# A three-layer graph network on one core: 13 extraction rounds, gathers over 104 partitions, and a reordered preparation

## The chip, the cores and the metric

The kernel runs on one core of one Trainium2 chip. The metric is the device time of one execution in microseconds. Five engines work side by side and wait for each other through semaphores: TensorE (PE), VectorE (DVE), ScalarE (ACT), GpSimd (POOL) and SyncE (SP, which issues most DMAs).

## The reference

A GraphSAGE network of three layers over 100000 nodes and 150000 edges (50000 drawn ones and one loop per node), sorted by destination. Neighbour rows are averaged over the in-degree.

```python
deg = segment_sum(ones, dst); inv_deg = where(deg > 0, 1 / maximum(deg, 1), 0)[:, None]
def sage(h, w_self, w_neigh, b):
    agg = segment_sum(h[src], dst) * inv_deg
    return h @ w_self + agg @ w_neigh + b
h = maximum(layernorm(x), 0)          # x: [100000, 128]
h = relu(sage(h, ws0, wn0, b0))       # 128 -> 256
h = relu(sage(h, ws1, wn1, b1))       # 256 -> 256
out = x + sage(h, ws2, wn2, b2)       # 256 -> 128
```

## The kernel before

**Tiles.** Nodes are cut into tiles of 128. Each node's own loop is handled apart, so that a tile has some 64 other edges. Layers 0 and 1 go over 392 pairs of tiles, layer 2 over 264 triples. For each tile one indirect DMA of GpSimd gathers the source rows of its edges, one edge per partition, and TensorE adds them up by destination with a 0/1 matrix (`select`). A partition with no edge has a row number out of bounds: its row is skipped, and what stands in the buffer (zeroed once) is multiplied by zero. Layer 0 gathers rows of `x` (512 bytes, L581), layer 1 rows of `p_rows` (1024 bytes, L595), layer 2 rows of `z_rows` (512 bytes, L608), two gathers per pair or triple. Buffers have four slots; each engine has its own hand-ordered loop.

**Preparation.** Ahead of layer 0 the kernel makes the edge lists. SyncE loads every 60th destination (`starts_b`, 2500 numbers copied to 114 partitions), the destinations (`dst_all`, `dst_next`), the weights and the biases. VectorE and ScalarE count, for seven chunks of 114 tiles each, where a tile's edges begin (`below`, `row_index`; ScalarE by the sum of a Sign, L638). GpSimd fetches a window of 300 edges per tile (`win_mem`, seven indirect DMAs of 114 rows, L519). Meanwhile the weights are split into two parts, `w_hi` by ScalarE (L641) and `w_lo` by VectorE (L848). Then each of a tile's edges gets a number (`wf_key`), 0 for foreign edges and own loops. Extraction takes the largest eight numbers of each tile with MAX8 (L874) and deletes them with MATCH_REPLACE8 (L878), seven tiles of chunks a round, `ROUNDS` = 14 rounds, so at most 112 edges a tile. TensorE turns the result (`keys`) so that edges lie on partitions. Out of it come `slot_index` (which row to gather), `slot_node` (which node in the tile it belongs to, from `node_i` and `empty_t`) and, for layer 2, the triple tables.

**The flag.** Six tests of the input (order, windows long enough, the last extracted slot empty, and so on) go into `faults`, are summed by TensorE, and set `general_flag`. If it is not 0, a slow general path for arbitrary inputs is taken. Each engine loads the flag and branches; GpSimd and ScalarE did so twice before layer 0, first around the general sums, then between the two forms of layer 0. SyncE's loads of `x`, GpSimd's gathers and all of layer 0 begin behind the flag.

Of the kernel before, what the change touches and what calls it, by code (L numbers as in the profile page):

```python
# [9 lines left out]
ALU = mybir.AluOpType  # L10
ACT = mybir.ActivationFunctionType
# [31 lines left out]
ROUNDS = 14  # L43
# [49 lines left out]
def build(nc, x, src, dst, dst_starts, windows, ws0, wn0, b0, ws1, wn1, b1, ws2, wn2, b2, out):  # L93
# [13 lines left out]
    with ExitStack() as ctx:  # L107
# [3 lines left out]
        def sem(name):  # L111
            return ctx.enter_context(nc.semaphore(name))
# [184 lines left out]
        prep = sem("prep")  # L297
        keys_ready, keys_taken, keys_turned = sem("keys_ready"), sem("keys_taken"), sem("keys_turned")
# [206 lines left out]
        def _(pool):  # L505
# [20 lines left out]

            def general(pass_no):
                table, sums, width = GENERAL[pass_no]
                with pool.If(pool.value_load(general_flag[0:1, 0:1], min_val=0, max_val=1) != 0):
                    if pass_no == 0:  # L530
                        pool.memset(zero_rows[:, :], 0.0).then_inc(ge_zero_made, 1)

                        pool.iota(slot_index[:, :], pattern=[[P, TILES]], base=0, channel_multiplier=1
                                  ).then_inc(ge_index_set, 1)
                    pool.wait_ge(ge_cleared, pass_no + 1)
                    with_degree = pass_no == 0
                    puts = 2 if with_degree else 1
                    with pool.Fori(0, EW) as i:
                        pool.wait_ge(ge_index, i + (pass_no * EW + 1))
                        pool.sem_inc(pool_may_go, 1)  # L540
                        pool.indirect_dma_start(ge_msg[:, 0:width], None, table,
                                                bass.IndirectOffsetOnAxis(ge_src[:, :], axis=0),
                                                bounds_check=last_row, oob_is_err=False).then_inc(ge_fetched[pass_no], 16)
                        pool.indirect_dma_start(ge_cur[:, 0:width], None, sums,
                                                bass.IndirectOffsetOnAxis(ge_at[:, :], axis=0),
                                                bounds_check=last_row, oob_is_err=False).then_inc(ge_fetched[pass_no], 16)
                        if with_degree:
                            pool.indirect_dma_start(ge_deg[:, :], None, degree_dram,
                                                    bass.IndirectOffsetOnAxis(ge_at[:, :], axis=0),
                                                    bounds_check=N_ROWS - 1, oob_is_err=False  # L550
                                                    ).then_inc(ge_fetched[pass_no], 16)
                        pool.wait_ge(ge_new_ready, i + (pass_no * EW + 1))
                        pool.sem_inc(pool_may_go, 1)
                        pool.indirect_dma_start(sums, bass.IndirectOffsetOnAxis(ge_put_at[:, :], axis=0),
                                                ge_new[:, 0:width], None,
                                                bounds_check=last_row, oob_is_err=False).then_inc(ge_put[pass_no], 16)
                        if with_degree:
                            pool.indirect_dma_start(degree_dram, bass.IndirectOffsetOnAxis(ge_put_at[:, :], axis=0),
                                                    ge_deg_new[:, :], None,
                                                    bounds_check=N_ROWS - 1, oob_is_err=False).then_inc(ge_put[pass_no], 16)  # L560
                        pool.wait_ge(ge_put[pass_no], i * (16 * puts) + 16 * puts)
                        pool.sem_inc(pool_may_go, 1)
                    if pass_no == 0:
                        pool.wait_ge(ge_index_set, 1)

            def layer0_gathers(table):
                def step(first):
                    if first.live():
                        if first.has(SLOTS):
                            pool.wait_ge(L0.gathered[first.slot], first.use * 32)  # L570
                        pool.tensor_copy(gather_at[first.slot][:, 0:2], slot_index[:, bass.ds(first.n * 2, 2)]
                                         ).then_inc(L0.index_copied, 1)
                    s = first.back(1)
                    if s.live():
                        if s.has(SLOTS):

                            pool.wait_ge(L0.normed, s.back(SLOTS).n + 1)
                        pool.wait_ge(L0.index_copied, s.n + 1)
                        pool.sem_inc(pool_may_go, 1)
                        for j in range(2):  # L580
                            pool.indirect_dma_start(raw[s.slot][:, 2 + j, :], None, table,  # L581
                                                    bass.IndirectOffsetOnAxis(gather_at[s.slot][:, j:j + 1], axis=0),
                                                    bounds_check=last_row, oob_is_err=False
                                                    ).then_inc(L0.gathered[s.slot], 16)
                pipeline(pool, step, PAIRS, 1)

            def gathers(layer, table, rows_in, freed, width):
                def gather(s):
                    if s.has(SLOTS):

                        pool.wait_ge(freed, s.back(SLOTS).n + 1)
                    pool.wait_ge(layer.index_copied, s.n + 1)
                    pool.sem_inc(pool_may_go, 1)
                    for j in range(2):
                        pool.indirect_dma_start(rows_in[s.slot][:, j, 0:width], None, table,  # L595
                                                bass.IndirectOffsetOnAxis(gather_at[s.slot][:, j:j + 1], axis=0),
                                                bounds_check=last_row, oob_is_err=False
                                                ).then_inc(layer.gathered[s.slot], 16)
                pipeline(pool, gather, PAIRS, 0)
# [32 lines left out]
        def _(act):  # L632
            act.wait_ge(const_made, 1)
            act.wait_ge(starts_loaded, 16)
# [17 lines left out]
            act.activation(wf_next, wf_loop, ACT.Copy, accum_out=loop_count[:, :]).then_inc(loops_counted, 1)  # L652

# [5 lines left out]
            act.wait_ge(flag_set, 1)  # L659
            with act.If(flagged()):  # L660
                with act.Fori(0, EW) as i:
                    act.wait_ge(ge_var_ready, i + 1)
                    act.activation(ge_std[:, :], ge_moments[:, 1:2], ACT.Sqrt, bias=eps_col[0:EP, :]
                                   ).then_inc(ge_std_ready, 1)
# [66 lines left out]
            act.wait_ge(nbr_cleared, SLOTS + 3)  # L731
            with act.If(flagged()):
                pipeline(act, layer0(True), PAIRS, 5)
                act.wait_ge(ge_nodes_off, 1)
# [60 lines left out]
        def _(dve):  # L795
# [86 lines left out]
            for j in range(SHARED):  # L882
                for q in range(SHARED_CHUNKS):
# [13 lines left out]
            own_step(dve.tensor_scalar(empty_t[:, :], keys_t[:, :], 0.0, -float(SENTINEL), op0=ALU.is_equal,  # L897
                                       op1=ALU.mult))

            dve.tensor_scalar(slot_index[:, :], key_i[:, :], 7, None, op0=ALU.logical_shift_right)  # L900
            own_step(dve.tensor_scalar(node_i[:, :], key_i[:, :], P - 1, None, op0=ALU.bitwise_and))
            own_step(dve.tensor_tensor(slot_node[:, :], node_i[:, :], empty_t[:, :], ALU.add))
# [11 lines left out]
            dve.reduce_max(faults[:, 5:6], shared_empty[:, :], AX.X).then_inc(faults_ready, 1)  # L914
            dve.wait_ge(faults_summed, 1)
# [4 lines left out]

            own_step(dve.tensor_tensor(keys_t[:, 0:n_own], keys_t[:, 0:n_own], shared_t[:, :], ALU.add))
# [503 lines left out]
```

## Time and profile before

| | us |
|---|---|
| median of 3 runs | 3935.56 |
| lowest, highest | 3934.75, 3937.95 |
| the profiled execution | 3934.27 |
| its span, first to last instruction | 3932.1 |
| preparation, to the first statistics of layer 0 | 142.2 |
| first and last gather of layer 1 start | 2165.4, 3214.8 |

Over the span PE is busy 3513.3 us (89%), DVE 3546.8 (90%), ACT 3016.1 (77%), POOL 2277.0 (58%). The granted TensorE clock is 0.933 of full speed in the mean; it is at full speed through layer 0.

How to read it: a row in order of time has the start in us from the span's start, the duration in us, the engine, the line, what it writes and reads, and in brackets how long the engine had been idle and what released it ("issue" means nothing that the profile shows). "x7" merges seven like instructions. SPq is SyncE's queue issuing a DMA; the row's duration is the issue, not the transfer. A DMA_INDIRECT row of POOL is the time in which GpSimd writes the gather's descriptors.

### The profile page before, as it was taken

What the parts mean: (1) busy time and instruction counts of PE and PEld (TensorE: products, weight loads), DVE (VectorE), ACT (ScalarE), POOL (GpSimd) and SP (SyncE); (2) the same over time, 40 slices, a digit from 0 to 9 for tenths busy, and PEclk for the clock granted to TensorE, in tenths of its full rate; (3) what the DMA queues carried; (4) which work ended last, traced back from release to release, by engine and by line L of the source; (5) the groups of instructions that cost most, each with busy time, mean ns of one, the idle gap of its engine ahead of it and who ended that gap; (6) DMA issues with size and microseconds to landing.
All of it is one profiled execution on the core that took longest, in us unless ns stands there. A gap on an engine that the chain in (4) does not pass through costs nothing. (4 is left out here: it accounts for less than half of the span.)

```text
span 3932.1 us, 111274 instructions
## 1 busy us (share of the span) xinstructions
PE 3513.3 (89%) x22511; PEld 3171.6 (81%) x22511; DVE 3546.8 (90%) x12529; ACT 3016.1 (77%) x8011; POOL 2277.0 (58%) x2513
## 2 busy tenths in 40 slices
PE   0499999999999999999999899999999987776666
PEld 0488888888888888888888799999999986666565
DVE  8899999999999999999998788888888877777777
ACT  2488888888888888888886778778778767777777
POOL 1344444444444444444442777777777767777776
PEclk9999999999999999999999999999999996666666
DMA  1144444444444444444444788888888878999998
GB/s 55 56 142 139 141 143 142 139 140 144 142 140 140 143 142 139 140 144 141 139 140 139 215 244 246 244 246 247 242 243 244 242 223 256 264 264 266 265 263 251
DMA packets 1040774, 727.06 MB, mean 185 GB/s; under 512 B 103208, under 2 KB 1012656, under 8 KB 1040632
## 3 DMA queue, kind: packets, MB, share of 16 engines
q1 hardware_dynamic: 854298, 569.93, 48.2%
q0 software_dynamic: 80848, 104.93, 10.7%
q10 hardware_dynamic: 105600, 51.92, 4.4%
q14 instruction: 22, 0.18, 0.0%
q8 instruction: 6, 0.10, 0.0%
HBM read 451.60 MB, written 360.71 MB: 207 GB/s over the span
## 5 line engine op out<-in xcount | busy, mean ns | idle before, releaser
L581 POOL DMA_INDIRECT loaded_rows<-in_x,gather_at x784 | 859.2, 1096 | 1047.6 <-ACT h_nbr L691 906.5
L1269 PE MATMUL ps_out<-w_hi,hid_hi 128*128 128x512 f32 (+1 forms) x3136 | 1120.6, 357 | 29.9 <-DVE layer_mem L1173 28.2
L1269 PE MATMUL ps_out<-w_hi,hid_lo 128*128 128x512 f32 (+1 forms) x3136 | 1066.3, 340 | 0.0
L1269 PE MATMUL ps_out<-w_lo,hid_hi 128*128 128x512 f32 (+1 forms) x3136 | 1061.9, 339 | 0.0
L595 POOL DMA_INDIRECT layer_mem<-p_rows,gather_at x784 | 804.1, 1026 | 289.2 <-issue 216.0
L1269 PEld LDWEIGHTS ps_out<-w_hi,hid_hi 128*128 128x128 f32 x3136 | 590.8, 188 | 139.4 <-issue 39.7
L1269 PEld LDWEIGHTS ps_out<-w_hi,hid_lo 128*128 128x128 f32 x3136 | 588.7, 188 | 72.5
L1269 PEld LDWEIGHTS ps_out<-w_lo,hid_hi 128*128 128x128 f32 x3136 | 592.8, 189 | 60.7
L608 POOL DMA_INDIRECT layer_mem<-z_rows,gather_at x528 | 525.8, 996 | 181.3 <-issue 140.8
L721 ACT ACTIVATE cat_hi<-ps_turn 128x512 fp32r<-128x512 f32 x392 | 236.0, 602 | 375.3 <-PE ps_turn L1306 373.9
L1269 PE MATMUL ps_hid<-cat_hi,w_hi 128*128 128x256 f32 x1568 | 472.0, 301 | 0.0
L780 ACT ACTIVATE layer_mem<-iota_row,triple_node 128x128 f32<-128x128 f32 x1056 | 337.3, 390 | 150.9 <-DVE stored_rows L1215 77.9
L1269 PE MATMUL ps_hid<-cat_lo,w_hi 128*128 128x256 f32 x1568 | 439.3, 280 | 0.0
L1269 PE MATMUL ps_hid<-cat_hi,w_lo 128*128 128x256 f32 x1568 | 438.9, 280 | 0.0
L1162 DVE SCALAR_TENSOR_TENSOR hid_lo<-ps_out,hid_hi 128x512 fp32r<-128x512 f32 x392 | 270.3, 690 | 111.0 <-ACT hid_hi L769 101.3
L691 ACT ACTIVATE h_own<-loaded_rows,shift,rstd 128x128 f32<-128x128 f32 x784 | 340.7, 484 | 2.0 <-DVE shift L1130 2.0
L1063 DVE BATCH_NORM_STATS2 stats<-loaded_rows 128x6 f32<-128x128 f32 x1568 | 338.1, 278 | 4.0 <-DMA loaded_rows<-in_x,gather_at 4.0
L691 ACT ACTIVATE h_nbr<-loaded_rows,shift,rstd 128x128 f32<-128x128 f32 x784 | 341.3, 484 | 0.0
L1107 DVE SCALAR_TENSOR_TENSOR layer_mem<-stored_rows,self_scale,ps_out 128x256 f32<-128x256 f32 x784 | 339.6, 475 | 0.1
L673 ACT ACTIVATE nbr_hi<-layer_mem 128x256 fp32r<-128x256 f32 x392 | 163.1, 416 | 229.9 <-DMA layer_mem<-p_rows,gather_at 227.4
L713 ACT ACTIVATE layer_mem<-ps_hid,b_col 128x256 f32<-128x256 f32 x784 | 320.7, 461 | 1.0 <-DVE hid_lo L1097 0.7
L1269 PEld LDWEIGHTS ps_hid<-cat_lo,w_hi 128*128 128x128 f32 x1568 | 296.6, 189 | 0.0
(162 smaller groups left out, 8783.6 us busy)
## 6 DMA issues: line engine op xcount, KB each, us to landing
p_rows<-stored_rows SPq DMA_DIRECT2D x392, 256.0 KB, 2.2
q_rows<-layer_mem SPq DMA_DIRECT2D x392, 256.0 KB, 2.6
loaded_rows<-q_rows SPq DMA_DIRECT2D x392, 256.0 KB
loaded_rows<-y_rows SPq DMA_DIRECT2D x264, 192.0 KB
layer_mem<-in_x SPq DMA_DIRECT2D x264, 192.0 KB
out_rows<-stored_rows ACTq DMA_DIRECT2D x264, 192.0 KB
loaded_rows<-in_x SPq DMA_DIRECT2D x392, 128.0 KB, 2.6
z_rows<-layer_mem SPq DMA_DIRECT2D x392, 128.0 KB
```

Source lines behind the costliest of these rows:

```text
L581: pool.indirect_dma_start(raw[s.slot][:, 2 + j, :], None, table, bass.IndirectOffsetOnAxis(gather_at[s.slot][:, j:j + 1], axis=0), bounds_ ...
L595: pool.indirect_dma_start(rows_in[s.slot][:, j, 0:width], None, table, bass.IndirectOffsetOnAxis(gather_at[s.slot][:, j:j + 1], axis=0), b ...
L608: pool.indirect_dma_start(triple_rows_in[s.slot][:, j, :], None, z_dram, bass.IndirectOffsetOnAxis(gather_at[s.slot][:, j:j + 1], axis=0), ...
L673: act.activation(nbr_hi[s.half][:, 0:tiles, 0:width], nbr[s.slot][:, 0:tiles, 0:width], ACT.Copy).then_inc(layer.nbr_hi_ready, 1)
L691: last = act.activation(rows, raw[t.slot][:, j, :], ACT.Relu, bias=shift[t.half][:, j:j + 1], scale=rstd[t.half][:, j:j + 1])
L713: last = act.activation(h1[t.half][:, m, :], ps_hid[t.half][:, m * PAIR:(m + 1) * PAIR], ACT.Relu, bias=b0_col[:, m:m + 1])
L721: act.activation(cat_hi[t.half][:, :, :], ps_turn[:, :].rearrange("p (k n) -> p k n", k=2), ACT.Copy).then_inc(L0.hi_ready, 1)
L780: last = act.activation(triple_distance[s.half][:, b, :], iota_row[:, :], ACT.Abs, scale=-1.0, bias=triple_node[:, bass.ds(s.n * (2 * SHAR ...
L1063: last = dve.bn_stats(stats[t.half][:, j, :], raw[t.slot][:, j, :])
L1107: last = dve.scalar_tensor_tensor(q_out[t.slot][:, j, :], p_out[t.slot][:, j, :], self_scale[:, bass.ds(t.n * 2 + j, 1)], ps_out[t.half][: ...
L1162: dve.scalar_tensor_tensor(hid_lo[t.half][:, :, :], l1_turn[t.half].rearrange("p (k n) -> p k n", k=2), 0.0, hid_hi[t.half][:, :, :].bitca ...
L1269: ins = nc.tensor.matmul(o, a, b, start=n == 0, stop=n == len(terms) - 1)
```

## The change

1. `ROUNDS` goes from 14 to 13; the gathers of layers 0 and 1 (plain path) take partitions 0 to `SLOT_ROWS` - 1 = 103 of the buffer and of the row numbers, where they took all 128. Layer 2 keeps 128.
2. SyncE waits for `starts_b` before it issues any other load. ScalarE runs a one-column Sign on an unused tile first.
3. ScalarE copies 342 of the 798 columns of `keys_t` beside VectorE's copy of 456. `empty_t` is made while TensorE sums the faults; `node_i` and `slot_node` are made behind the flag.
4. GpSimd and ScalarE test the flag once before layer 0: the general sums move into the branch that chooses the form of layer 0. (`general_sums` is the old body of `general`, unchanged.)

```diff
-ROUNDS = 14
+ROUNDS = 13
+SLOT_ROWS = 8 * ROUNDS
@@ sync
             sp.dma_start(starts_b, ...).then_inc(starts_loaded, 16)
+            sp.wait_ge(starts_loaded, 16)
             sp.dma_start(dst_all[:, :], dst_flat).then_inc(dst_loaded, 16)
@@ gpsimd: layer0_gathers(table, rows), gathers(...)
-                            pool.indirect_dma_start(raw[s.slot][:, 2 + j, :], None, table,
-                                                    bass.IndirectOffsetOnAxis(gather_at[s.slot][:, j:j + 1], axis=0),
+                            pool.indirect_dma_start(raw[s.slot][0:rows, 2 + j, :], None, table,
+                                                    bass.IndirectOffsetOnAxis(gather_at[s.slot][0:rows, j:j + 1], axis=0),
...
-                        pool.indirect_dma_start(rows_in[s.slot][:, j, 0:width], None, table,
+                        pool.indirect_dma_start(rows_in[s.slot][0:SLOT_ROWS, j, 0:width], None, table,
...
-            general(0)
             with pool.If(pool.value_load(general_flag[0:1, 0:1], min_val=0, max_val=1) != 0):
-                layer0_gathers(h0_sums)
+                general_sums(0)
+                layer0_gathers(h0_sums, P)
             with pool.Else():
-                layer0_gathers(x)
+                layer0_gathers(x, SLOT_ROWS)
@@ scalar
             act.wait_ge(const_made, 1)
+            act.activation(ge_alone[:, :], eps_col[:, :], ACT.Sign)
             act.wait_ge(starts_loaded, 16)
...
+            act.wait_ge(keys_turned, 1)
+            act.activation(keys_t[:, 4 * TP:TILES], l1_turn[1][:, 0:(CHUNKS - 4) * TP], ACT.Copy).then_inc(keys_copied, 1)
@@ vector
-            dve.tensor_copy(keys_t[:, 0:4 * TP], l1_turn[0][:, 0:4 * TP])
-            own_step(dve.tensor_copy(keys_t[:, 4 * TP:TILES], l1_turn[1][:, 0:(CHUNKS - 4) * TP]))
-            dve.tensor_scalar(key_i[:, :], keys_t[:, :], -1.0, None, op0=ALU.add)
+            own_step(dve.tensor_copy(keys_t[:, 0:4 * TP], l1_turn[0][:, 0:4 * TP]))
+            dve.wait_ge(keys_copied, 1)
+            own_step(dve.tensor_scalar(key_i[:, :], keys_t[:, :], -1.0, None, op0=ALU.add))
```

VectorE from the turned keys to the flag (L918 before, L923 after), before:

```order
L894 COPY keys_t<-ps_out 128x456 [waits keys_turned]
L895 COPY keys_t<-ps_out 128x342
L896 TENSOR_SCALAR key_i<-keys_t 128x798 [waits prep]
L897 TENSOR_SCALAR empty_t<-keys_t 128x798
L900 TENSOR_SCALAR slot_index<-key_i 128x798 [waits prep]
L901 TENSOR_SCALAR node_i<-key_i 128x798
L902 TENSOR_TENSOR slot_node<-node_i,empty_t 128x798 [waits prep]
...
L912 SCALAR_TENSOR_TENSOR layer_mem<-keys_t,layer_mem 128x528 [waits prep]
L914 TENSOR_REDUCE faults<-layer_mem 128x1 [waits prep]
L916 TENSOR_REDUCE fault_sum<-ps_out 128x1 [waits faults_summed]
L917 TENSOR_SCALAR fast<-fault_sum 128x1 [waits prep]
L918 TENSOR_SCALAR general_flag<-fault_sum 1x1
```

and after:

```order
L902 COPY keys_t<-ps_out 128x456 [waits keys_turned]
L904 TENSOR_SCALAR key_i<-keys_t 128x798 [waits keys_copied,prep]
L905 TENSOR_SCALAR slot_index<-key_i 128x798 [waits prep]
L912 COPY layer_mem<-ps_hid 128x264 [waits shared_turned]
L912 COPY layer_mem<-ps_hid 128x264
L915 SCALAR_TENSOR_TENSOR layer_mem<-keys_t,layer_mem 128x528 [waits prep]
L917 TENSOR_REDUCE faults<-layer_mem 128x1 [waits prep]
L918 TENSOR_SCALAR empty_t<-keys_t 128x798
L921 TENSOR_REDUCE fault_sum<-ps_out 128x1 [waits faults_summed,prep]
L922 TENSOR_SCALAR fast<-fault_sum 128x1 [waits prep]
L923 TENSOR_SCALAR general_flag<-fault_sum 1x1
```

`empty_t` stands behind the instruction that hands the faults to TensorE, `node_i` and `slot_node` behind the flag, and one copy of two is gone.

GpSimd from the window gathers to the first gather of layer 0 (left out are the general path and its form of layer 0), before:

```order
L529 TENSOR_LOAD general_flag [waits nbr_cleared,flag_set]
L529 ISA x2
L529 COMPARE_AND_BRANCH
...
L616 TENSOR_LOAD general_flag
L616 ISA x2
L616 COMPARE_AND_BRANCH
...
L616 UNCONDITIONAL_BRANCH
L571 COPY gather_at<-slot_index 128x2 x2
L581 DMA loaded_rows<-in_x,gather_at 128x128 [waits index_copied_0]
L581 DMA loaded_rows<-in_x,gather_at 128x128
```

and after:

```order
L621 TENSOR_LOAD general_flag [waits nbr_cleared,flag_set]
L621 ISA x2
L621 COMPARE_AND_BRANCH
...
L621 UNCONDITIONAL_BRANCH
L577 COPY gather_at<-slot_index 128x2 x2
L587 DMA loaded_rows<-in_x,gather_at 104x128 [waits index_copied_0]
L587 DMA loaded_rows<-in_x,gather_at 104x128
```

One load of the flag with its branch is gone, and the gather writes 104 partitions.

SyncE's first loads, before:

```order
L395 DMA layer_mem<-in_dst_starts 114x2500
L397 DMA dst_all<-in_dst 125x1200
L398 DMA dst_next<-in_dst 124x2
L399 DMA b_col<-in_L_gnn_b 128x2x1
L400 DMA layer_mem<-in_L_gnn_ws 128x256
```

and after:

```order
L397 DMA layer_mem<-in_dst_starts 114x2500
L400 DMA dst_all<-in_dst 125x1200 [waits starts_loaded]
L401 DMA dst_next<-in_dst 124x2
L402 DMA b_col<-in_L_gnn_b 128x2x1
L403 DMA layer_mem<-in_L_gnn_ws 128x256
```

The second load now waits for the first to land.

## Rows read from the trace of the kernel before

**Rows 1.** Busy time per engine (count), TensorE clock, DMA; layers 0, 1.

```profile
400.00:2150.00 1750.00, 1750.00 (x10964) 1560.36 (x10963) 1724.41 (x6821) 1418.89 (x3759) 806.16 (x1013) 1.00 0.47 141
2250.00:3200.00 950.00, 924.32 (x7087) 870.42 (x7086) 844.35 (x2481) 757.64 (x2125) 726.65 (x708) 1.00 0.84 245
```

**Rows 2.** GpSimd's gathers by line: busy, mean ns, idle before; last row min/median/max ns.

```profile
L581 POOL DMA_INDIRECT loaded_rows<-in_x,gather_at x674 | 740.0, 1098 | 914.9 <-ACT h_nbr L691 795.0 <-issue 113.9 <-POOL gather_at L571 6.0
...
L595 POOL DMA_INDIRECT layer_mem<-p_rows,gather_at x708 | 726.7, 1026 | 223.5 <-issue 156.2 <-DVE gather_at L1027 44.4 <-PE ps_hid L1341 12.2
...
L595 POOL DMA_INDIRECT layer_mem<-p_rows,gather_at x784: 992/998/1340, 2165.4 to 3214.8; - x196
```

**Rows 3.** In order of time: start, us, engine, line; VectorE, two extraction rounds.

```profile
82.35 2.69 DVE L874 MAX8 keys<-wf_key_mem 114x8 f32<-114x300 f32 x7
...
88.03 2.69 DVE L874 MAX8 keys<-wf_key_mem 114x8 f32<-114x300 f32 x7
```

**Rows 4.** In order of time, the first 32 us, several engines.

```profile
11.23 2.82 DVE L831 TENSOR_SCALAR_CACHE_REDUCE layer_mem<-layer_mem,tile_base 114x2500 f32<-114x2500 int32 x1 [6.00 <-DMA layer_mem<-in_dst_starts]
...
11.27 1.28 ACT L638 ACT_TABLE_LOAD   x1 [11.27 <-DMA layer_mem<-in_dst_starts]
...
13.67 1.26 SPq L406 DMA_DIRECT2D layer_mem<-in_L_gnn_ws  x1
...
15.07 0.15 DVE L828 TENSOR_SCALAR row_index<-below 114x1 int32<-114x1 f32 x1 [0.64 <-ACT layer_mem L638]
...
22.46 1.89 ACT L641 ACTIVATE w_hi<-layer_mem 128x2048 fp32r<-128x2048 f32 x1
...
27.10 2.29 DVE L848 TENSOR_TENSOR w_lo<-layer_mem,w_hi 128x2048 fp32r<-128x2048 f32 x1
...
31.68 2.35 DVE L854 TENSOR_TENSOR layer_mem<-win_mem 114x2100 f32<-114x2100 int32 x1 [2.28 <-DMA win_mem<-in_windows,row_index]
```

**Rows 5.** DMA view, 0:12 and 12:32 us: packets, MB; us to landing.

```profile
q1 hardware_dynamic: 551, 1.54, 36.8%
...
layer_mem<-in_L_gnn_ws SPq DMA_DIRECT2D x1, 128.0 KB, 6.0
```

**Rows 6.** In order of time, VectorE from keys to flag.

```profile
127.10 0.50 DVE L895 COPY keys_t<-ps_out 128x342 f32<-128x342 f32 x1
...
128.13 0.57 DVE L897 TENSOR_SCALAR empty_t<-keys_t 128x798 f32<-128x798 f32 x1
...
129.83 0.99 DVE L902 TENSOR_TENSOR slot_node<-node_i,empty_t 128x798 f32<-128x798 int32 x1
...
133.80 0.17 DVE L916 TENSOR_REDUCE fault_sum<-ps_out 128x1 f32<-128x8 f32 x1 [0.69 <-PE ps_out L1238]
...
134.07 0.13 DVE L918 TENSOR_SCALAR general_flag<-fault_sum 1x1 int32<-1x1 f32 x1
```

**Rows 7.** In order of time, from flag to first pair of layer 0.

```profile
135.29 2.14 SPq L464 DMA_DIRECT2D loaded_rows<-in_x  x4
...
136.37 0.70 POOL L571 COPY gather_at<-slot_index 128x2 int32<-128x2 int32 x2 [108.31 <-issue]
...
137.58 1.84 POOL L581 DMA_INDIRECT loaded_rows<-in_x,gather_at  x1 [0.51 <-POOL gather_at L571]
...
139.73 1.00 POOL L581 DMA_INDIRECT loaded_rows<-in_x,gather_at  x1 [0.30 <-issue]
...
142.22 0.87 DVE L1063 BATCH_NORM_STATS2 stats<-loaded_rows 128x6 f32<-128x128 f32 x4 [3.59 <-DMA loaded_rows<-in_x,gather_at]
```

**Rows 8.** In order of time, GpSimd, the last window gather.

```profile
26.88 1.19 POOL L519 DMA_INDIRECT win_mem<-in_windows,row_index  x1 [0.30 <-issue]
```

**Rows 9.** Gather queue's packets, MB: 400:2150, 2250:3200, 12:32 us.

```profile
q0 software_dynamic: 21600, 22.24, 6.0%
...
q0 software_dynamic: 33978, 46.60, 18.7%
...
q0 software_dynamic: 1232, 1.92, 32.0%
```

More of the change, by code:

```diff
@@ L297, in build @@
         prep = sem("prep")
+        keys_copied = sem("keys_copied")
         keys_ready, keys_taken, keys_turned = sem("keys_ready"), sem("keys_taken"), sem("keys_turned")
@@ L525, in _, with general_sums @@
             last_row = pool.snap(limit)
+            def general_sums(pass_no):
+                table, sums, width = GENERAL[pass_no]
+                if pass_no == 0:
+                    pool.memset(zero_rows[:, :], 0.0).then_inc(ge_zero_made, 1)
+                    pool.iota(slot_index[:, :], pattern=[[P, TILES]], base=0, channel_multiplier=1
+                              ).then_inc(ge_index_set, 1)
+                pool.wait_ge(ge_cleared, pass_no + 1)
+                with_degree = pass_no == 0
+                puts = 2 if with_degree else 1
+                with pool.Fori(0, EW) as i:
+                    pool.wait_ge(ge_index, i + (pass_no * EW + 1))
+                    pool.sem_inc(pool_may_go, 1)
+                    pool.indirect_dma_start(ge_msg[:, 0:width], None, table,
+                                            bass.IndirectOffsetOnAxis(ge_src[:, :], axis=0),
+                                            bounds_check=last_row, oob_is_err=False).then_inc(ge_fetched[pass_no], 16)
+                    pool.indirect_dma_start(ge_cur[:, 0:width], None, sums,
+                                            bass.IndirectOffsetOnAxis(ge_at[:, :], axis=0),
+                                            bounds_check=last_row, oob_is_err=False).then_inc(ge_fetched[pass_no], 16)
+                    if with_degree:
+                        pool.indirect_dma_start(ge_deg[:, :], None, degree_dram,
+                                                bass.IndirectOffsetOnAxis(ge_at[:, :], axis=0),
+                                                bounds_check=N_ROWS - 1, oob_is_err=False
+                                                ).then_inc(ge_fetched[pass_no], 16)
+                    pool.wait_ge(ge_new_ready, i + (pass_no * EW + 1))
+                    pool.sem_inc(pool_may_go, 1)
+                    pool.indirect_dma_start(sums, bass.IndirectOffsetOnAxis(ge_put_at[:, :], axis=0),
+                                            ge_new[:, 0:width], None,
+                                            bounds_check=last_row, oob_is_err=False).then_inc(ge_put[pass_no], 16)
+                    if with_degree:
+                        pool.indirect_dma_start(degree_dram, bass.IndirectOffsetOnAxis(ge_put_at[:, :], axis=0),
+                                                ge_deg_new[:, :], None,
+                                                bounds_check=N_ROWS - 1, oob_is_err=False).then_inc(ge_put[pass_no], 16)
+                    pool.wait_ge(ge_put[pass_no], i * (16 * puts) + 16 * puts)
+                    pool.sem_inc(pool_may_go, 1)
+                if pass_no == 0:
+                    pool.wait_ge(ge_index_set, 1)
@@ L527, in general @@
             def general(pass_no):
-                table, sums, width = GENERAL[pass_no]
                 with pool.If(pool.value_load(general_flag[0:1, 0:1], min_val=0, max_val=1) != 0):
[L530 to L564, printed above, removed]
@@ L566, in layer0_gathers @@
-            def layer0_gathers(table):
+                    general_sums(pass_no)
+            def layer0_gathers(table, rows):
                 def step(first):
@@ L652, in _ @@
             act.activation(wf_next, wf_loop, ACT.Copy, accum_out=loop_count[:, :]).then_inc(loops_counted, 1)
+            act.wait_ge(keys_turned, 1)
+            act.activation(keys_t[:, 4 * TP:TILES], l1_turn[1][:, 0:(CHUNKS - 4) * TP], ACT.Copy).then_inc(keys_copied, 1)
             def flagged():
                 return act.value_load(general_flag[0:1, 0:1], min_val=0, max_val=1) != 0
[L659 to L664, printed above, removed]
             def nbr_hi_part(layer, s, tiles, width):
@@ L731, in _ @@
             act.wait_ge(nbr_cleared, SLOTS + 3)
+            act.wait_ge(flag_set, 1)
             with act.If(flagged()):
+                with act.Fori(0, EW) as i:
+                    act.wait_ge(ge_var_ready, i + 1)
+                    act.activation(ge_std[:, :], ge_moments[:, 1:2], ACT.Sqrt, bias=eps_col[0:EP, :]
+                                   ).then_inc(ge_std_ready, 1)
                 pipeline(act, layer0(True), PAIRS, 5)
@@ L914, in _ @@
             dve.reduce_max(faults[:, 5:6], shared_empty[:, :], AX.X).then_inc(faults_ready, 1)
+            own_step(dve.tensor_scalar(empty_t[:, :], keys_t[:, :], 0.0, -float(SENTINEL), op0=ALU.is_equal,
+                                       op1=ALU.mult))
             dve.wait_ge(faults_summed, 1)
@@ L919, in _ @@
             dve.sem_inc(flag_set, 1)
+            own_step(dve.tensor_scalar(node_i[:, :], key_i[:, :], P - 1, None, op0=ALU.bitwise_and))
+            own_step(dve.tensor_tensor(slot_node[:, :], node_i[:, :], empty_t[:, :], ALU.add))
             own_step(dve.tensor_tensor(keys_t[:, 0:n_own], keys_t[:, 0:n_own], shared_t[:, :], ALU.add))
```

6 lines of the change are left out of this document (1 added, 5 removed).

## Prediction

> **What bounds the kernel now.** I read the busy time by stage first, then the gathers' own lines, then the first 145 us in order of time, because the change touches the preparation and the gathers and nothing else. [rows 1] gives the two long stages. In layer 0 TensorE is busy 1750.00 of 1750.00 us, at full clock: it is the bound. In layer 1 TensorE is busy 924.32 of 950.00 us and GpSimd 726.65. That looks like TensorE again, but [rows 2] says otherwise. GpSimd's 708 gathers took 726.7 us and the gaps between them 223.5 us, 950.2 together, so GpSimd never stops in layer 1. The gap is the same 0.3 us after each (223.5 / 708 = 0.316), an issue cost and no wait. The 784 gathers of the layer start between 2165.4 and 3214.8 us, one each 1.34 us. So a hundredth of a microsecond on one layer 1 gather is 7.8 us of kernel. In layer 0 GpSimd is idle 914.9 of 1750 us, most of it waiting for ScalarE to free a buffer: there the gather's length costs nothing. Layer 2 keeps its 128 partitions and is left alone. Ahead of layer 0 stands the preparation, some 142 us of a serial chain through VectorE, in which each step saved comes off the end.
>
> **One round of extraction.** A round is seven MAX8 and seven MATCH_REPLACE8, back to back with no idle time. It starts at 82.35 and the next at 88.03 [rows 3]: 5.68 us. The 14th goes: **-5.7**. The wider zero fill of `keys` is a part of a 0.15 us memset. The limit falls from 111 edges a tile to 103; counted from the inputs, the fullest of the 782 tiles has 89 edges besides its nodes' own loops, so the flag stays 0 and the plain path runs.
>
> **Row numbers alone and first.** VectorE starts its first count at 11.23 us after 6.00 us of idle time, on the landing of `starts_b` [rows 4]. By 12 us the queue had moved 1.54 MB [rows 5], and `starts_b` is 114 x 2500 x 4 bytes, 1.14 MB: at most 0.40 MB of other data went before its end or just behind it. At the mean of 1.54 MB in 12 us that is worth 3.1 us if all of it was in the way, and nothing if it was queued behind. SyncE issued `starts_b` first and one queue serves its transfers in turn, so I take a value near the lower end, **-0.5**, and keep 0 to -2 for the range (some of the 0.40 MB certainly fell in the last microsecond). Below nothing it can't go: nothing new stands ahead of this load.
>
> What is pushed back are the eleven other loads and the padding store; they now start at about 11 us. Before, the last weight load was issued at 13.67 [rows 4] and landed 6.0 us later [rows 5], and its issue had stood behind the big loads draining. With `starts_b` gone I expect it at 16 to 17 us, landed at 22 to 23; at worst it keeps its distance and is issued 11 us later, at 24.7, landed at 30.7. ScalarE is free for `w_hi` at 22.46, or 21.4 with what follows. VectorE takes `w_lo` at 27.10 and idles 2.28 us before the windows come at 31.68 [rows 4]. With 1.89 us for `w_hi` and 2.29 for `w_lo`, both fit if the weights land by 26.4: cover for the likely case, not for the worst, which costs 4.3.
>
> **The table load.** The first Sign of ScalarE loads its table for 1.28 us after the row numbers have come, at 11.27 [rows 4]. The dummy Sign on `ge_alone` does it while ScalarE waits anyway. VectorE waited 0.64 us for the first ScalarE count, at 15.07; later counts were ready. **-0.6**, passed on through `row_index`, GpSimd's seven window gathers and their landing, since the last gather, not the weights, ends the wait at 31.68.
>
> **The way to the flag.** Four steps leave it. The copy L895 (0.5) goes to ScalarE beside VectorE's wider copy; at ScalarE's rate for `w_hi`, 1.89 us for 2048 columns [rows 4], its 342 columns end sooner. `empty_t` L897 (0.6) goes into the 0.69 us in which VectorE waits for the fault sum. `node_i` L901, of the shape of L897, and `slot_node` L902 (0.6 and 1.0) go behind the flag [rows 6]. That is 2.7; what had been overlapped between short instructions and is now a wait costs some 0.2: **-2.5**, the flag at 131.7 where it was 134.2 (on the old clock).
>
> **Behind the flag.** SyncE's first load goes out 1.09 us after the flag (134.20 to 135.29) with one test of the flag; GpSimd's index copy 2.17 us after it (136.37) with two [rows 7]. The merged branch leaves GpSimd one test: **-1.1**. Against it: the first gather took 1.84 us and the second 1.00; beside the first VectorE was making the node tables, beside the second it had stopped at 138.63 [rows 7]. Now `node_i` and `slot_node` fill the gap and both gathers lie beside VectorE, so the second may take 1.84 too: 0 to +0.84, **+0.4**. (The Trainium skill, "SBUF — State Buffer", section "Who interferes with whom", says that VectorE's two-port modes lock GpSimd out of writing descriptors; these two rows agree, the 0.84 us above is theirs.) VectorE is done with its tables at 131.7 + 1.6 + 4.4 = 137.7, before the first pair lands at about 139, so the tables are covered; if the gathers came 1 us sooner they would not be. ScalarE's merged branch ends in idle time.
>
> Sum of the preparation: -5.7 - 0.5 - 0.6 - 2.5 - 1.1 + 0.4 = **-10.0 us**, from -8.3 (row numbers 0, gather +0.84, 0.8 of waits more) to -12. Layers 0 to 2 then run as they did.
>
> **104 partitions.** The rows with no edge carry an index out of range and fetch nothing, before as after, so no bytes go. What could change is GpSimd's time to write a gather. The trace has one other size, the window gathers of 114 rows: 1.19 us against a median of 0.998 [rows 2, 8]. Fewer rows took longer. The queue's packets explain it [rows 9]. Layer 0: 21600 over 674 gathers, 32 = 16 x 2. Layer 1: 33978 over 708, 48 = 16 x 3. Windows: 1232 over 7, 176 = 16 x 11. One of each engine's packets is the completion; the others are 1, 2 and 10, which fit eight rows of 512 bytes, eight of 1024 and 19 of 2400 at up to 4 to 5 KB a packet. So all 16 engines always get a list as long as that of the one with the most rows, and 114 rows were dealt as 6 x 19, where 16 x 8 would have held them. Dealt evenly, 104 is 13 x 8: the list stays at 8. GpSimd's time goes with the list (0.19 us for 11 entries more, 0.017 each), and so stays at 1.00: **0 us** for 784 gathers.
>
> The Trainium skill ("DMA: Bandwidth & Descriptors", section "Why a DMA increments its semaphore by 16 and not by 1", paragraph "How many engines (k)") states the rule outright: the largest k up to 16 that divides the number of partitions. The packet counts agree with it for 114 and 128; no run so far shows 104. By the common reading, that fewer partitions mean less work, the sum would be the -28 us of the first rival below; by this rule it is the -10.0.
>
> The profiled execution took 3934.27 us, span 3932.1; the median of the runs is 3935.56, 1.3 more. 3935.56 - 10.0 = **3925.6 us**.
>
> **Rivals.** *Gathers get shorter.* If time goes with rows or with a list of 104/16, 6.5 rounded to 7, a gather saves 0.017 us (-13 us, 3912), and in proportion to the rows up to 0.19. It can't all be had: TensorE is idle only 25.7 of 950 us of layer 1 [rows 1], 2.7%, so it takes over as the bound after 28 us: 3898. For: nothing but the smaller number. Against: the 114 rows.
>
> *Gathers get longer*, the one that ends slower. Part of the 0.19 us of the window gathers may be not the longer list but the uneven deal itself, a path of the descriptor writer for anything but 16 engines. Layer 1 pays it 784 times with no cover, layer 0 not at all. At 0.013 us it has eaten the 10.0; at the full 0.19 it is +149, 4075. Were 104 dealt as 8 x 13, the list of 13 would give 5 x 0.017 x 784 = +67, 3993. Against: the arithmetic of a list explains the 0.19 alone.
>
> *The preparation gives less.* The loads pushed back meet the window gathers on the queue's engines, and the last window or the weights land 2 to 8 us late (the weights' worst is 4.3): 3928 to 3934. For: weights, edge ends and windows now share 12 to 25 us. Against: the cover above.
>
> **How the numbers follow.** Forecast 0.50 (3923 to 3928). Shorter gathers 0.14, longer 0.22 (a third of it below +30), less preparation 0.14. A measurement of this kernel tells about 0.2% from no change, 7.9 us: faster is below 3927.7. Most of the forecast, the shorter gathers and a little of the last case give 0.60; the last case, the edge of the forecast and a loss of 0.003 to 0.02 us per gather give 0.22; beyond that 0.18. The range takes the forecast, less preparation, shorter gathers to -20 and longer ones to +0.025: **3905 to 3943**.
>
> **What would show it.** In the trace after: rounds still 5.68 us, twelve replaces; ScalarE's table load before 5 us and no 0.64 us wait; flag 9.3 us sooner than 134.2; first statistics at about 132.2 instead of 142.22; layer 1 gathers at a median of 1.00 and one each 1.34 us; the gather queue's packets still 32 and 48 a gather. I am wrong if the layer 1 median moves by over 0.01 us, if the packets a gather change, or if the windows land later than 30.8.

## The result: slower by 1.0%, and the profile after

| | before | changed |
|---|---|---|
| median us | 3936.35 | 3976.19 |
| lowest, highest | 3934.75, 3937.95 | 3974.81, 3978.92 |
| span of the profiled run | 3932.1 | 3976.7 |

The ratio is 1.0102, with a 95% interval of 1.0085 to 1.012: 40 us lost, where 10 gained were forecast. The range ended at 3943. (The column "before" has one run more than the table ahead of the prediction, and with it a median 0.8 us higher.)

The busy times by stretch of the changed kernel, columns as in [rows 1], the first row layer 0, the second layer 1:

```profile
390.00:2140.00 1750.00, 1750.00 (x10967) 1559.71 (x10966) 1724.79 (x6826) 1419.49 (x3760) 833.13 (x1016) 1.00 0.47 141
...
2250.00:3200.00 950.00, 899.93 (x6774) 826.39 (x6772) 814.72 (x2371) 723.05 (x2028) 742.15 (x677) 1.00 0.83 234
```

Layer 0 is as it was: TensorE has no idle time. In layer 1 TensorE fell from 924.32 to 899.93 us of 950, VectorE and ScalarE fell too, and GpSimd rose. The gathers of the changed kernel (layer 0's line, layer 1's line with shortest, median and longest ns and the start of first and last; then layer 1's busy time, mean and idle time before) stand against [rows 2]:

```profile
L587 POOL DMA_INDIRECT loaded_rows<-in_x,gather_at x784: 1076/1090/1254, 129.0 to 2111.5; - x196
...
L601 POOL DMA_INDIRECT layer_mem<-p_rows,gather_at x784: 1077/1082/1432, 2157.3 to 3258.7; - x196
...
L601 POOL DMA_INDIRECT layer_mem<-p_rows,gather_at x677 | 743.2, 1098 | 208.1 <-issue 147.0 <-DVE gather_at L1034 49.2 <-PE ps_hid L1348 6.7
```

The median gather of layer 1 went from 0.998 to 1.082 us, the shortest from 0.992 to 1.077. GpSimd still never stops: 743 us of work and 208 of gaps fill the stretch. First to last start is now 1101.4 us where it was 1049.4: **+52.0**. The first gather of layer 1 starts at 2157.3 instead of 2165.4: **-8.1** from what stands before. The span grew by 44.6, and 52.0 - 8.1 is 43.9 of it.

The gather queue's packets in the same two stretches (packets, MB, share), against [rows 9]:

```profile
q0 software_dynamic: 21632, 22.27, 6.6%
...
q0 software_dynamic: 32458, 44.49, 19.6%
```

Layer 1: 32458 packets over 677 gathers, 47.9 each; 48.0 before. The bytes are the same too, 65.7 and 65.8 KB a gather. By both the queue carries the same lists; the time in which GpSimd writes them is longer.

The preparation of the changed kernel in order of time, against [rows 3, 4, 6, 7]:

```profile
10.56 2.82 DVE L839 TENSOR_SCALAR_CACHE_REDUCE layer_mem<-layer_mem,tile_base 114x2500 f32<-114x2500 int32 x1 [5.33 <-DMA layer_mem<-in_dst_starts]
...
25.71 1.20 POOL L522 DMA_INDIRECT win_mem<-in_windows,row_index  x1 [0.30 <-issue]
...
25.88 1.91 ACT L648 ACTIVATE w_hi<-layer_mem 128x2048 fp32r<-128x2048 f32 x1 [5.33 <-DMA layer_mem<-in_L_gnn_ws]
...
31.87 2.35 DVE L862 TENSOR_TENSOR layer_mem<-win_mem 114x2100 f32<-114x2100 int32 x1 [1.68 <-DMA win_mem<-in_windows,row_index]
...
116.68 2.69 DVE L882 MAX8 keys<-wf_key_mem 114x8 f32<-114x300 f32 x7
...
125.89 0.17 DVE L921 TENSOR_REDUCE fault_sum<-ps_out 128x1 f32<-128x8 f32 x1 [0.27 <-PE ps_out L1245]
...
126.17 0.13 DVE L923 TENSOR_SCALAR general_flag<-fault_sum 1x1 int32<-1x1 f32 x1
...
127.73 0.48 POOL L577 COPY gather_at<-slot_index 128x2 int32<-128x2 int32 x2 [100.82 <-issue]
...
129.01 1.21 POOL L587 DMA_INDIRECT loaded_rows<-in_x,gather_at  x1 [0.79 <-POOL gather_at L577]
...
130.53 1.22 POOL L587 DMA_INDIRECT loaded_rows<-in_x,gather_at  x1 [0.30 <-issue]
...
133.70 0.87 DVE L1070 BATCH_NORM_STATS2 stats<-loaded_rows 128x6 f32<-128x128 f32 x4 [1.32 <-DMA loaded_rows<-in_x,gather_at]
```

### The profile page after: what moved, and what is told of

Same layout as the page of the kernel before. It is cut to its first block and busy times, and to the rows that moved or that the text cites. A ratio compares the mean times of both kernels' runs of the same rounds, so it can differ in the third digit from the quotient of the medians.

```text
span 3976.7 us, 111247 instructions
## 1 busy us (share of the span) xinstructions
PE 3532.3 (89%) x22511; PEld 3167.0 (80%) x22511; DVE 3549.9 (89%) x12507; ACT 3016.5 (76%) x8013; POOL 2364.0 (59%) x2513
## 5 line engine op out<-in xcount | busy, mean ns | idle before, releaser
L587 POOL DMA_INDIRECT loaded_rows<-in_x,gather_at x784 | 890.2, 1136 | 1014.8 <-ACT h_nbr L694 874.2
L1276 PE MATMUL ps_out<-w_hi,hid_hi 128*128 128x512 f32 (+1 forms) x3136 | 1111.5, 354 | 59.4 <-DVE layer_mem L1180 55.9
L601 POOL DMA_INDIRECT layer_mem<-p_rows,gather_at x784 | 860.9, 1098 | 284.3 <-issue 216.2
```

The source lines that it names most:

```text
L587: pool.indirect_dma_start(raw[s.slot][0:rows, 2 + j, :], None, table, bass.IndirectOffsetOnAxis(gather_at[s.slot][0:rows, j:j + 1], axis=0 ...
L601: pool.indirect_dma_start(rows_in[s.slot][0:SLOT_ROWS, j, 0:width], None, table, bass.IndirectOffsetOnAxis(gather_at[s.slot][0:SLOT_ROWS, ...
L1276: ins = nc.tensor.matmul(o, a, b, start=n == 0, stop=n == len(terms) - 1)
```

## Experiments

Two theories stood against each other on the gather. **A**: the loss is in the gather over 104 partitions alone, and in it a price for any number of partitions that isn't dealt over all 16 DMA engines. **Rivals**: something else in the change slows layer 1; or any gather over fewer than 128 partitions pays; or the price goes with the number of engines left out.

### Both gathers back at 128 partitions

```diff
-SLOT_ROWS = 8 * ROUNDS
+SLOT_ROWS = P
```

> The changed kernel with the gathers of layers 0 and 1 back over 128 partitions, all else kept. Theory A (the loss is the gather over 104 partitions and nothing else): layer 1 median back at 0.998 us, one gather each 1.34 us, its 784 gathers in 1050 us where the changed kernel took 1102; time 3976 - 52 = 3924 to 3928, which is before less the 8.5 us that the preparation gained. Rival (something else of the change, such as the shorter preparation or the merged branch, slows layer 1): the gathers stay near 1.08 us and the time near 3970.

Measured: 4350.61 us where the kernel before took 4359.51, ratio 0.998 (0.997 to 0.9989). These times need a word. This run, the kernel with eight sizes and the first runs with 112 and with 96 partitions were on another chip, on which layers 1 and 2 took longer. Layer 1's gathers and one of its waits there:

```profile
L601 POOL DMA_INDIRECT layer_mem<-p_rows,gather_at x784: 992/998/1345, 2156.6 to 3484.2; - x196
...
ACT layer_mem L768 <- DMA y_rows<-layer_mem: 113.7, 101, 3.1
```

The gather is back at 0.998 us, but the layer's 784 start over 1328 us, GpSimd is idle for 587 us of them, and ScalarE waits for the stores of `y_rows`: there GpSimd does not set the pace. (The waits on the stores point to the memory; no run isolates it.) The gather's length can be read there, its price can't. So the kernel ran again on a chip like the first:

> The kernel with both gathers at 128 again, because the first time its layer 1 took 1328 us instead of 1050, in the kernel before as well, waiting for stores: there the gather was not the bound. Theory A, where layer 1 goes at the gathers' pace: before less 8 to 9 us, and 1050 us for the 784 gathers.

3927.09 us where before took 3935.72, ratio 0.9977 (0.9967 to 0.9987). Layer 1's gathers, and the longest of ScalarE's waits from 2250 to 3200 us:

```profile
L601 POOL DMA_INDIRECT layer_mem<-p_rows,gather_at x784: 992/998/1348, 2156.8 to 3207.1; - x196
...
ACT nbr_hi L676 <- DMA layer_mem<-p_rows,gather_at: 190.1, 267, 3.2
```

Here ScalarE waits for the gathers, and never for the stores of `y_rows`.

The gathers take 1050.3 us from first to last start, 1049.4 before the change. Theory A holds to a microsecond: with 128 partitions and all else of the change the loss is gone, and what is left is the preparation's gain, 8.6 us.

### Layer 0 alone at 104

```diff
-pool.indirect_dma_start(rows_in[s.slot][0:SLOT_ROWS, j, 0:width], None, table,
-                        bass.IndirectOffsetOnAxis(gather_at[s.slot][0:SLOT_ROWS, j:j + 1], axis=0),
+pool.indirect_dma_start(rows_in[s.slot][:, j, 0:width], None, table,
+                        bass.IndirectOffsetOnAxis(gather_at[s.slot][:, j:j + 1], axis=0),
```

> The changed kernel with layer 1's gathers back over 128 partitions and layer 0's kept at 104. Theory A: layer 0 gathers stay at 1.09 us but GpSimd waits there for ScalarE anyway, so no time is lost: as the kernel with both at 128, 0.2% below before, 3924 to 3928 where before is 3936. Rival (layer 0 pays too, by its share): 784 x 0.084 = 66 us more.

3925.58 us, ratio 0.9974 (0.9963 to 0.9986), 1.5 us from the kernel with both at 128 on the same chip, which is inside the spread of the runs.

```profile
L587 POOL DMA_INDIRECT loaded_rows<-in_x,gather_at x784: 1076/1090/1253, 128.5 to 2111.4; - x196
...
L601 POOL DMA_INDIRECT layer_mem<-p_rows,gather_at x784: 992/998/1346, 2157.1 to 3205.1; - x196
```

Layer 0's gathers are as long as in the changed kernel and cost nothing, as its 874 us of waiting for ScalarE said. The whole loss is layer 1's 784.

### Which numbers of partitions pay

One kernel with eight numbers in layer 1, each on its own line:

```diff
+if s.slot == 0:
+    pool.indirect_dma_start(*one(0, 128), **more).then_inc(done, 16)
+    pool.indirect_dma_start(*one(1, 120), **more).then_inc(done, 16)
+elif s.slot == 1:
+    ... one(0, 112), one(1, 104)
+elif s.slot == 2:
+    ... one(0, 96), one(1, 114)
+else:
+    ... one(0, 98), one(1, 100)
```

> One look. Layer 1's eight gathers of a round of four slots each over another number of partitions, each on a line of its own: 128, 120, 112, 104, 96, 114, 98, 100; layer 0 over 128. Lists by an even deal: 16x8, 15x8, 16x7, 13x8, 16x6, 6x19, 14x7, 10x10. A1: medians 1.00, 1.08, 0.99, 1.08, 0.98, 1.19, 1.07, 1.10. A2: all but the first 1.07 or more. If the price went with idle engines (13 of 16 gave 0.084, 0.028 each): 120 at 1.03, 98 at 1.05, 100 at 1.18.

Shortest, median and longest, in the order 128, 120, 112, 104, 96, 114, 98, 100:

```profile
L606 POOL DMA_INDIRECT layer_mem<-p_rows,gather_at x98: 1007/1035/1142, 2157.3 to 3463.6; - x98
...
L607 POOL DMA_INDIRECT layer_mem<-p_rows,gather_at x98: 1067/1349/1421, 2158.7 to 3464.9; - x98
...
L609 POOL DMA_INDIRECT layer_mem<-p_rows,gather_at x98: 1019/1023/1028, 2160.0 to 3467.6; - x98
...
L610 POOL DMA_INDIRECT layer_mem<-p_rows,gather_at x98: 1065/1069/1377, 2161.4 to 3468.9; - x98
...
L612 POOL DMA_INDIRECT layer_mem<-p_rows,gather_at x98: 993/999/1010, 2162.8 to 3470.3; - x98
...
L613 POOL DMA_INDIRECT layer_mem<-p_rows,gather_at x98: 1187/1441/1454, 2164.0 to 3471.6; - x98
...
L615 POOL DMA_INDIRECT layer_mem<-p_rows,gather_at x98: 1038/1042/1047, 2165.5 to 3474.4; - x98
...
L616 POOL DMA_INDIRECT layer_mem<-p_rows,gather_at x98: 1057/1061/1182, 2166.9 to 3475.7; - x98
```

The gather queue's packets over the layer:

```profile
q0 software_dynamic: 43792, 51.51, 16.8%
```

By the shortest times 128, 112 and 96 are 1.01, 1.02 and 0.99, and those that aren't multiples of 16 are 1.04 to 1.07, with 114 at 1.19 as for the windows. That fells the rival that any number under 128 pays. Against the rival of the engines left out, 120 was no nearer to 128 than 104 was. Against theory A's expectation too, 98 and 100 were shorter than 104, and 100 although its list (10 rows) is longer than that of 104 (8) and more engines are left out: the surcharge follows neither alone. The 114 at 1.19 has rows of 1024 bytes here and had 2400 among the windows, so the width of a row is not in it. Medians mislead here: the longer gather among them fell almost only on two lines, 120 and 114 (70 and 77 of their 98). Mixed, 96, 112 and 128 also take 0.035 us more in the median than alone, and 104 takes 0.013 less, so the sizes had to be run each by itself.

The packets say how the rows were dealt. By the prediction's reading each of 16 engines gets one packet for every four rows of its list and one more: 48 packets for a list of up to eight, 64 for ten, 96 for nineteen. Dealt by the largest divisor up to 16, the eight sizes make 56.0 a gather in the mean; dealt over all 16, they would make 48. It was 43792 / 784 = 55.9. So 100 and 114 partitions were dealt unevenly; for 104, 120 and 98 both ways of dealing give 48, and the count can't tell.

Each by itself:

```diff
-SLOT_ROWS = 8 * ROUNDS
+SLOT_ROWS = 120        # and, in other kernels, 98 and 112
```

> Gathers of layers 0 and 1 over 120 partitions, 15 x 8: the list is as long as with 128 and 104, one engine idle. A1 (a fixed price for any number not dealt over all 16): median 1.08 us, layer 1 at 1102 us, time 3972 to 3978. Rival by idle engines (0.084 us for three, 0.028 each): 1.026 us, time 3946.

> Gathers of layers 0 and 1 over 98 partitions, 14 x 7: an uneven deal with a list one shorter than 104 and two engines idle. A1: 1.06 to 1.08 us a gather. By idle engines: 1.05 and less for the shorter list, 1.04. If fewer rows or a shorter list could pay for the uneven deal it would be under 1.00.

> The changed kernel with the gathers over 112 partitions (13 rounds kept). Theory A1 (a fixed price of some 0.08 us for a number that is not dealt over all 16 engines, and a small price per entry of the longest list): 112 is 16 x 7, so 0.99 us a gather, time 3915 to 3927. Rival A2 (any gather over fewer than 128 partitions pays 0.08 us): 1.07 to 1.09 us, time 3970 to 3977.

> Gathers over 112 partitions (16 x 7), 13 rounds, again, where layer 1 goes at the gathers' pace. Its median was 0.992 us, 0.006 below the 0.998 of 128: 784 x 0.006 = -5 us against 128, so before less 9 and 5, about 3921. A2 (any number under 128 pays) would give 3976.

Layer 1's gathers for 120, 98 and 112 partitions, each alone:

```profile
L601 POOL DMA_INDIRECT layer_mem<-p_rows,gather_at x784: 1077/1082/1439, 2157.0 to 3260.1; - x196
...
L601 POOL DMA_INDIRECT layer_mem<-p_rows,gather_at x784: 1038/1043/1392, 2156.5 to 3231.9; - x196
...
L601 POOL DMA_INDIRECT layer_mem<-p_rows,gather_at x784: 982/988/1332, 2158.1 to 3196.9; - x196
```

Each ratio is to the kernel before on the run's own chip; the deals are those of the largest divisor:

| partitions | deal | median us | time | ratio to before |
|---|---|---|---|---|
| 96 (12 rounds) | 16 x 6 | 0.964 | 3900.67 | 0.9907 (0.989 to 0.9923) |
| 112 | 16 x 7 | 0.988 | 3919.11 | 0.9957 (0.9941 to 0.9974) |
| 128 | 16 x 8 | 0.998 | 3927.09 | 0.9977 (0.9967 to 0.9987) |
| 98 | 14 x 7 | 1.043 | 3951.82, one run | |
| 120 | 15 x 8 | 1.082 | 3980.34 | 1.0112 (1.0095 to 1.0128) |
| 104, the change | 13 x 8 | 1.082 | 3976.19 | 1.0102 (1.0085 to 1.012) |

120 and 104 agree to the nanosecond, with one engine left out and with three: the price doesn't go with engines left out, nor with rows. (120 took 3980.34 us, a little above theory A's 3972 to 3978 and far from the rival's 3946. At 98 that rival had 1.04 us and was met, theory A had 1.06 to 1.08 and missed; 120 is what fells the rival.) With the same list, the uneven deal costs 0.084 us at 8 entries (1.082 against 0.998) and 0.055 at 7 (1.043 against 0.988). (On the other chip 112 gave 4353.42 us, ratio 0.9985, 0.9976 to 0.9995, where the gather had no say.) Theory A holds in its place; that the surcharge is one fixed number doesn't. What is shown is that five sizes that 16 does not divide cost more and three that it divides don't (100 and 114 only in the kernel with eight sizes). That the deal over the engines is the cause is the reading that fits the packets; 13 x 8 isn't seen in any row, and no run parts the deal from some other property of multiples of 16.

### 96 partitions and 12 rounds

The fullest tile has 89 edges, so that 96 slots still hold every tile.

```diff
-ROUNDS = 13
+ROUNDS = 12
```

> 12 rounds of extraction and gathers over 96 partitions (the fullest tile has 89 edges, so the output is whole). Theory A1: 96 is 16 x 6, two entries fewer than 128; with the price per entry from the window gathers, (1.19 - 1.084) / 11 = 0.0096 us, 0.98 us a gather, -15 us in layer 1, and -5.7 us for the round: 3904 to 3908. With 0.017 us an entry as the prediction had it: 0.964 us, 3894. A2: 1.08 us, 3968.

> 12 rounds and 96 partitions again. Its gathers took a median of 0.964 us. Where layer 1 goes at the gathers' pace: 784 x 0.034 = -27 us if TensorE lets it (its idle time in layer 1 was 26 of 950 us, so -20 to -28), -5.7 us for the round and -8.5 for the rest of the preparation: before less 34 to 42 us, 3894 to 3902 where before is 3936.

On the other chip 4361.06 us, ratio 1.0001 (0.9992 to 1.0011): neither the shorter gather nor the round brought anything that could be measured there. On the first kind of chip 3900.67, **35 us less than before**, faster than both kernels. It lies inside the expected 3894 to 3902. Layer 1's gathers, their busy and idle time with 96 and with 128, and the stretch with 96:

```profile
L601 POOL DMA_INDIRECT layer_mem<-p_rows,gather_at x784: 958/964/1317, 2150.6 to 3185.5; - x196
...
L601 POOL DMA_INDIRECT layer_mem<-p_rows,gather_at x784 | 779.2, 994 | 299.5 <-issue 247.4 <-DVE gather_at L1034 31.3 <-PE ps_hid L1348 8.2
...
L601 POOL DMA_INDIRECT layer_mem<-p_rows,gather_at x784 | 804.2, 1026 | 290.0 <-issue 225.9
...
2250.00:3180.00 930.00, 912.47 (x7040) 868.96 (x7038) 836.58 (x2465) 755.33 (x2112) 697.94 (x705) 1.00 0.88 248
```

The median is 0.034 us below 128's, 27 us over the layer, and not the 0.02 that theory A took from the window gathers (0.98 us); first to last start is 1034.9 us, 15.4 less than with 128. GpSimd's work fell by 25 us (779.2 from 804.2), but its idle time rose by 9.5 (299.5 from 290.0), with TensorE busy 912 of 930 us. The ceiling that [rows 1] showed is near, but that TensorE holds the gathers back isn't shown: GpSimd's waits on VectorE and TensorE did not grow (34.8 and 10.4 us in 900 us of the layer with 128, 27.5 and 7.0 in 930 us with 96), only the gaps with no releaser ("issue") did, from 225.9 to 247.4 us.

### The preparation

> The changed kernel with gathers at 128 and without SyncE's wait for the row numbers, the other parts of the preparation kept. Theory P: VectorE starts its count at 11.2 again instead of 10.55, 0.64 us is saved by the table load, and the windows land 3.6 to 4.1 us after the last gather's issue, at 31.0 to 31.3, no later than with the wait (mean of eight profiles 31.6); w_hi starts at 21.9. Rival (the wait brings its 0.67 us): the windows land 0.7 us later than with the wait, at 32.2. In time both within 0.1% of the kernel with the wait and 128, 3927.

```diff
 sp.dma_start(starts_b, ...).then_inc(starts_loaded, 16)
-sp.wait_ge(starts_loaded, 16)
 sp.dma_start(dst_all[:, :], dst_flat).then_inc(dst_loaded, 16)
```

VectorE's first count, GpSimd's last window gather and VectorE's first work on the windows, without the wait:

```profile
11.31 2.82 DVE L838 TENSOR_SCALAR_CACHE_REDUCE layer_mem<-layer_mem,tile_base 114x2500 f32<-114x2500 int32 x1 [6.08 <-DMA layer_mem<-in_dst_starts]
...
26.46 1.18 POOL L521 DMA_INDIRECT win_mem<-in_windows,row_index  x1 [0.30 <-issue]
...
31.58 2.35 DVE L861 TENSOR_TENSOR layer_mem<-win_mem 114x2100 f32<-114x2100 int32 x1 [2.60 <-DMA win_mem<-in_windows,row_index]
```

With the wait the same three stood at 10.56, 25.71 and 31.87 in the changed kernel. The count starts 0.75 us later without it, the last gather is issued 0.75 us later, and the windows land at 31.58: later than theory P's 31.0 to 31.3 and sooner than the rival's 32.2. Eleven profiles with the changed preparation (the changed kernel and the ten runs above) have that landing between 31.01 and 32.40, 31.63 in the mean. In these profiles the wait's 0.7 us don't arrive: **no gain from loading the row numbers alone can be seen**. One profile without the wait against a spread of 1.4 us doesn't prove it by the landing itself. The way from the end of the last issue to the landing says more: 3.6 us before and 3.9 here, and 4.2 to 5.4 in each of the eleven with the wait. The time, 3925.09 us (ratio 0.9968, 0.9955 to 0.998), agrees with the 3927.09 of the kernel with the wait. A suspect was the padding store, which now runs beside the windows:

```diff
-sp.wait_ge(const_made, 1)            # in the order of the loads
-sp.dma_start(y_dram[N_ROWS:N_PAD, :]...).then_inc(padding_stored, 16)
+... the same two lines behind sp.wait_ge(flag_set, 1) and general(0)
```

> Both gathers at 128, and the padding store of SyncE (512 KB) moved behind the flag, so that it does not run beside the window gathers. Theory P (the sooner start of the counts was lost because what was pushed back meets the window gathers): windows land 0.6 to 1.1 us sooner, VectorE's L862 row at 30.2 to 31.0 where five profiles of the changed preparation had 31.0 to 32.3, mean 31.7. Rival Q (the landing varies by itself, the store does not matter): 31.0 to 32.3 again. In time 1 us at most, not to be measured; the row decides.

```profile
31.12 2.35 DVE L862 TENSOR_TENSOR layer_mem<-win_mem 114x2100 f32<-114x2100 int32 x1 [1.72 <-DMA win_mem<-in_windows,row_index]
```

31.12, inside the spread of the others, though near its lower end; 3926.77 us (0.9973, 0.996 to 0.9985). The way from issue to landing, 4.2 us, is at the lower end too. This decides nothing: one profile against a spread of 1.4 us. The windows took longer to land in all twelve profiles in which the loads were pushed back beside them; that these loads are the cause is likely and not shown, and which of them is open.

## Why the prediction was wrong

**The step that failed** stands under the 104 partitions: "GpSimd's time goes with the list (0.19 us for 11 entries more, 0.017 each), and so stays at 1.00: 0 us". One pair of points, 128 and 114 partitions, was given wholly to the length of the list, although the two gathers differed in length, in evenness and in the width of a row. The second rival said just that, with the right mechanism and place: "the uneven deal itself, ... Layer 1 pays it 784 times with no cover, layer 0 not at all". It was given a chance of 0.22, but set against the forecast with the argument that the list explains the 0.19 alone, which it did no better than the deal; and the range took it in only up to 0.025 us a gather. At 104 the surcharge is 0.084 us. How the 0.19 of 114 partitions splits into list and deal isn't shown, since the surcharge was 0.084 at lists of eight and 0.055 at lists of seven. The term of 0 is +52 us: GpSimd's work in layer 1 rose by 57 us (860.9 for 804.1), less 5 us of shorter gaps.

**What held of it.** The bound of layer 1 (GpSimd, without a pause), the 7.8 us for each 0.01 us of gather, layer 0's indifference and the unchanged 48 packets. Of its three signs of being wrong two came: the median of layer 1 moved by 0.084 us, and the windows landed at 31.87, not by 30.8. The ceiling of 28 us for shorter gathers stays undecided: 96 partitions brought 15.4 us in layer 1, with TensorE still idle 17.5 of 930 us. By the second rival's own arithmetic 0.084 us is 66 us; the mean gather rose by less, 0.072, since fewer were long: 45 of the 784 took over 0.15 us more than the median, where 74 did before.

**The preparation**, -10.0 forecast, is -8.5 by the first statistics (142.22 to 133.70) and -8.6 by the kernel with 128, inside the -8.3 to -12 it was given. By its steps, -5.6 + 0.2 - 2.5 - 0.6:

- The round: -5.7 forecast. From the windows to the last round's first MAX8 it is 84.81 us; before, with that MAX8 at 122.11, it was 90.43: -5.6. Right.
- Row numbers first and the table load: -0.5 and -0.6 forecast, the count 0.67 us sooner (10.56 for 11.23), ScalarE's count no longer waited for, the last window gather at 25.71 for 26.88. All of the 1.17 us is gone at the windows' landing, 31.87 for 31.68. This is the rival "the preparation gives less", in a milder form than its 2 to 8 us. The gathers were issued sooner and landed later: 3.6 us from the end of the last issue to VectorE's start before, 4.96 in the changed kernel. Why is open, as above.
- The weights: `w_hi` began at 25.88, not at 22 to 23; the cover worked out for it, 26.4, was just enough. VectorE still idled 1.68 us ahead of the windows.
- The way to the flag: -2.5 forecast. From the last round's MAX8 to the flag it is 9.62 us (116.68 to 126.30) and was 12.09: -2.47. Right; `empty_t` took the wait for the fault sum down from 0.69 to 0.27 us.
- Behind the flag: -1.1 for the test, +0.4 for the gathers beside VectorE. GpSimd's copy comes 1.43 us after the flag, 2.17 before: -0.7. Both first gathers took 1.2 us, where one had taken 1.84 and one 1.00, -0.4 together, and the rows landed later, 1.95 us from the end of the second issue to the statistics where it was 1.49: +0.5. From flag to statistics it is 7.40 for 8.02 us, -0.6 where -0.7 was forecast. The sum was right, its parts less so: beside VectorE's table work neither gather took the 1.84 us that the prediction had read from one row as VectorE's doing, although the second ran in part beside the same VectorE instruction on `triple_node` (L939, at 131.30). That reading isn't borne out.

## What to carry to other kernels

Where GpSimd's gathers follow each other without a pause, their issue time is the kernel's time, and among the sizes tried the partition count of a gather is chosen by whether 16 divides it, not by how small it is: 112 or 96 shortened it, 104, 120 and 98 lengthened it, all with the same rows fetched. And a single odd point in a trace can't be given to one of two differences at once; when the price is paid 784 times, each reading of it belongs in the range.

## What the runs showed of the hardware

- An indirect gather over 96, 112 and 128 partitions took GpSimd 0.964, 0.988 and 0.998 us, over 98, 104 and 120 partitions 1.043, 1.082 and 1.082. The steps aren't even: 0.024 from 96 to 112, 0.010 from 112 to 128.
- Some layer 1 gathers took up to 0.36 us more than the median in every kernel (1.340 against 0.998 us in the kernel before), so that the mean is 0.03 above it with 128 and with 96 partitions, and only 0.016 with 104, where fewer are long. What makes them long is open.
- Two chips differed by 424 us on the kernel before (4359.51 and 3935.72 us). In the profiles of the kernel with 128 partitions from both, all of the difference lies in layers 1 and 2 (layer 1 begins at 2156.6 and 2156.8 us), with stores of `y_rows` waited for on the slower one. The 12 rounds and 96 partitions were worth 35 us on the one and nothing that could be measured on the other.
